# Late weight pieces rounded on ScalarE, an earlier read of the logits, the first gate mix by chunk, and a tile's Gram products between projections

## What is computed

```
L0 attention (gated delta rule, 4 heads of 32, chunks of 32 tokens):
  q, k, v = silu(conv4(x @ W.T))            # k and q then scaled to unit length
  beta = sigmoid(x @ Wb.T)
  attn = -(beta*k @ k.T) strictly lower; row by row: attn[i] += attn[i] @ attn; attn += I
  per chunk: u_new = attn @ (beta*v) - (attn @ (beta*k)) @ S
             o = q @ S + causal(q @ k.T) @ u_new;  S += k.T @ u_new
  mix = sigmoid(x @ Wmix.T);  o = mix*o + (1-mix)*v;  rms norm;  @ Wo.T
L0 feed-forward: top 2 of 8 experts by logits x @ router_w.T, softmax of the two as gate,
                 out = sum_e gate[e] * (gelu(x @ w1[e].T) @ w2[e].T)
L1 attention (linear recurrence): a = exp(-8 softplus(a_param) sigmoid(xWa)), y = scan(a, b)
L1 feed-forward: silu(xW1)*(xW2) -> gelu(.H1) -> gelu(.H2) -> W3     (128 -> 512 -> 128)
```

## Time and profile before

| | us |
|---|---|
| median of 3 runs | 802.26 |
| lowest | 798.42 |
| profiled execution | 804.78 |
| its span | 803.0 |

### The profile page before, as it was taken

One profiled execution on the slowest core, in us unless ns is written; L12 is line 12 of the kernel. 1 busy time (PEld: TensorE's weight loads), 2 busy tenths in 40 slices (PEclk: granted clock), 3 DMA queues, 4 the chain that ended last, 5 costly groups with the idle time before them and its releaser, 6 DMA issues.

```text
span 803.0 us, 11422 instructions
## 1 busy us (share of the span) xinstructions
PE 759.0 (95%) x3525; PEld 581.9 (72%) x3525; DVE 576.1 (72%) x1150; ACT 498.2 (62%) x799; POOL 491.5 (61%) x504
## 2 busy tenths in 40 slices
PE   8999999989979799999989999999999999999996
PEld 5777786777667567766777778767867787777775
DVE  5786788697669677687777777777777677776553
ACT  6877645335945565567557755774577467677753
POOL 0069699279988565987586347544754474386343
PEclk9999899789999899999999999999999999999998
DMA  4135526323131400141014002301230120021000
GB/s 144 54 106 146 168 70 180 108 80 96 37 115 51 112 14 27 53 105 28 27 53 133 27 27 63 95 26 29 63 94 24 40 65 13 1 82 39 0 14 13
DMA packets 47820, 52.68 MB, mean 66 GB/s; under 512 B 2784, under 2 KB 32224, under 8 KB 47776
## 3 DMA queue, kind: packets, MB, share of 16 engines
q1 hardware_dynamic: 47776, 52.13, 22.4%
HBM read 38.62 MB, written 13.50 MB: 65 GB/s over the span
## 4 chain that ended last, share of the span: by engine, by line
PE 67%; DVE 11%; POOL 8%; issue 6%; ACT 5%; DMA 2%; SPq 0%; DVEq 0%; ACTq 0%; POOLq 0%
PE bank L466 67%; POOL fbl L1370 3%; POOL acc L1378 2%; DVE spread L1631 1%; POOL tmp L1311 1%; POOL tpm L1314 1%; DVE sexp L1639 1%; DVE m L1688 1%; DVE x L1622 1%; DVE fbl L1838 1%; POOL texp L1338 1%; DVE yg L1649 1%; DMA conv<-in_conv 1%; DVE x3h L1855 1%; POOL fbl L1413 1%
## 5 line engine op out<-in xcount | busy, mean ns | idle before, releaser
L1370 POOL TENSOR_TENSOR fbl<-hf,fbh 128x512 fp32r<-128x512 f32 x64 | 90.2, 1409 | 40.8 <-ACT fbh L1161 40.4
L1149 ACT ACTIVATE hf<-bank 128x512 f32<-128x512 f32 x64 | 38.2, 598 | 123.0 <-PE bank L466 101.1
L1311 POOL TENSOR_TENSOR tmp<-apm,tpm 128x31 f32<-128x31 f32 (+15 forms) x124 | 73.5, 593 | 42.5 <-DVE apm L1503 34.4
L1838 DVE TENSOR_TENSOR fbl<-hf,fbh 128x512 fp32r<-128x512 f32 x64 | 69.2, 1082 | 39.4 <-ACT fbh L1155 37.1
L1314 POOL TENSOR_TENSOR tpm<-tpm,tmp 128x31 f32<-128x31 f32 (+15 forms) x124 | 77.1, 622 | 9.7
L1378 POOL TENSOR_TENSOR acc<-acc,yg 128x512 f32<-128x512 f32 x48 | 69.8, 1454 | 21.1 <-DVE yg L1649 21.1
L1413 POOL TENSOR_TENSOR fbl<-hf,fbh 128x512 fp32r<-128x512 f32 x28 | 37.0, 1324 | 72.6 <-DVE fbh L1905 72.6
L466 PE MATMUL bank<-fal,wfh 128*128 128x512 f32 x160 | 67.8, 423 | 0.0
L466 PE MATMUL bank<-fbl,wmh 128*128 128x512 f32 x128 | 60.0, 469 | 8.0 <-POOL fbl L1370 5.0
L466 PE MATMUL bank<-fah,wfh 128*128 128x512 f32 x160 | 62.5, 390 | 0.0
L466 PE MATMUL bank<-fah,wfl 128*128 128x512 f32 x160 | 62.2, 389 | 0.0
(11 more groups left out here) (246 smaller groups left out, 2155.6 us busy)
## 6 DMA issues: line engine op xcount, KB each, us to landing
gb<-gt SPq DMA_DIRECT2D x64, 256.0 KB, 3.2
pk<-pack SPq DMA_DIRECT2D x7, 1280.0 KB, 7.1
pack<-pk SPq DMA_DIRECT2D x5, 1280.0 KB, 6.9
ws<-in_wf SPq DMA_DIRECT2D x11, 256.0 KB, 2.8
pack<-pk SPq DMA_DIRECT2D x4, 640.0 KB, 4.0
xs<-in_xh SPq DMA_DIRECT2D x8, 262.0 KB, 2.8
xt<-in_xh SPq DMA_DIRECT2D x8, 262.0 KB, 2.9
ws<-in_wm SPq DMA_DIRECT2D x8, 256.0 KB, 3.3
```

Source lines behind the costliest of these rows:

```text
L1149: A.activation(hf[:, 0, :], bank[4][:, :], ACT.Gelu).then_inc(S["gelu_done"], 1)
L1311: G.tensor_tensor(m, a, r, ALU.mult).then_inc(S["t_mul"], 1)
L1370: G.tensor_tensor(fbl[:, sl, :], hf[:, 1, :], f32(fbh[:, sh, :]), ALU.subtract)\
L1838: tt(fbl[:, sl, :], hf[:, 0, :], f32(fbh[:, sh, :]), ALU.subtract).then_inc(S["lo0"], 1)
```

## The change

```diff
 def piece_high(pieces):                      # ScalarE, new
+    for p in pieces:
+        act.wait_ge(*loaded(p))
+        A.activation(high_of(p), buf_of(p)[:, :], ACT.Copy).then_inc(S["ws_act"], 1)
 
 split_pieces (VectorE):
-    V.tensor_copy(high_of(p), buf_of(p)[:, :]).then_inc(S["ws_hi"], 1)
-    dve.wait_ge(S["ws_hi"], p + 1)
+    if p < BY_SCALAR:                        # BY_SCALAR = 9
+        V.tensor_copy(high_of(p), buf_of(p)[:, :]).then_inc(S["ws_hi"], 1)
+        dve.wait_ge(S["ws_hi"], p + 1)
+    else:
+        dve.wait_ge(S["ws_act"], p - BY_SCALAR + 1)
 
 tiles 0 to 4 (TensorE):
     else:
         project(t + 1, 0)
+        project(t + 1, 1)
     gram(t, 0)
+    if t + 1 == LEAD:
+        project(t + 1, 2)
     gram(t, 1)
 ramp1 (TensorE):
-    project(s, 1)
     delta_in(a, 0)
...
     delta_turn(a, 0)
-    project(s, 2)
 
 ramp1 (ScalarE):
     heads_in(s, 1)
+    heads_in(s, 2)
...
     A.preload_act_table_set(SILU)
-    heads_in(s, 2)
+    piece_high(PIECES[s - 1][:2])
     delta_g(a, 2)
+    piece_high(PIECES[s - 1][2:])
     heads_in(s + 1, 0)
     heads_in(s + 1, 1)
+    piece_high(PIECES[s])
     delta_g(a, 3)
 ramp2 (ScalarE):
     attention_square(a)
+    piece_high(PIECES[s][:2])
     rstd_ln("1", a, 2, a4)
 ramp3 (ScalarE):
     key_spread(s, 0)
+    key_spread(s, 1)
     lru_root(m)
 dense (ScalarE), behind the activations of expert e:
+    if first and m == 0 and e in (0, 1, 3, 5):
+        p = (0, 1, 3, 5).index(e)
+        piece_high((PIECES[NT - 2][2:] + PIECES[NT - 1])[p:p + 1])
 
 VectorE:
+def mix_chunk(a, n):
+    part = lambda ap: ap.rearrange("p (b n c) -> p b n c", b=B, n=CN)[:, :, n, :]
+    if n == 0:
+        dve.wait_ge(*after("mix_act", a + 1))
+    dve.wait_ge(*after("o_copied", CN * a + n + 1))
+    stt(part(a3[:, :]), part(a4[:, :]), 1.0, part(a3[:, :]), ALU.add, ALU.mult).then_inc(S["mix_o"], 1)
+    dve.wait_ge(S["mix_o"], CN * a + n + 1)
+    i = stt(part(a1[:, :]), part(a3[:, :]), 0.5, pk[:, n:CT:CN, SV, :], ALU.mult, ALU.add)
+    if n == CN - 1:
+        i.then_inc(S["o_ready"], 1)
 ramp1 (VectorE):
     split_x(s + 1)
+    mix_chunk(a, 0)
...
     delta_out(a, 1)
+    mix_chunk(a, 1)
...
     delta_out(a, 2)
+    mix_chunk(a, 2)
...
     delta_out(a, 3)
-    mix(a)
-    mix_end(a)
+    mix_chunk(a, 3)
 ramp3 (VectorE):
     attention_low(a)
+    logits(a)                                # the copy that top_two began with
     unit_rows(s)
     lru_m(m)
-    dve.wait_ge(S["kq_done"], 2 * s + 2)
-    tt(kspread[slot(s)][1], rep(pks[s][:, 8:16, SK:SK + 1, :], 2, NH), heads(8), ALU.mult)\
-        .then_inc(S["kexp_dve"], 1)
-    top_two(a)
+    top_two(a, False)
```

More of the change, by code:

```diff
@@ L175, in loaded @@
             return S[f"ws_in{PIECE_BUF[p]}"], 16 * (PIECE_BUF[:p].count(PIECE_BUF[p]) + 1)
+        BY_SCALAR = NM + 1
         CENTRED = tuple(range((WM - O_DN) // PIECE)) + (NM,)
@@ L187, in low_of @@
             return part_of(p, wml, wfl)
-        names = """w_in cst_in conv_in0 conv_in1 conv_in2 x_in pk_half pk_stored pk_loaded tb_in fw_in ws_in0 ws_in1 ws_hi ws_lo warm_in xs_in tt_stored
+        names = """w_in cst_in conv_in0 conv_in1 conv_in2 x_in pk_half pk_stored pk_loaded tb_in fw_in ws_in0 ws_in1 ws_hi ws_act ws_lo warm_in xs_in tt_stored
             ws_sum ws_mean ws_cen s3_row s3_read cen_ready w3_scaled wo_sum wo_mean wo_cen
             wtap_f wtap_hi wtap_done xt_hi xt_ready
-            beta_proj qkv_proj qkv_act sq_done ss_done rs_ln rs_act kq_done kt_done kexp_done kexp_dve gram_done
+            beta_proj qkv_proj qkv_act sq_done ss_done rs_ln rs_act kq_done kt_done kexp_done gram_done
             bt_ready beta_tmp beta_tok_done gram_read
@@ L523, in gram @@
                 pe.wait_ge(S["kq_done"], 2 * t + 2)
-                if t == NT - 1 and g:
-                    pe.wait_ge(S["kexp_dve"], 1)
-                else:
-                    pe.wait_ge(S["kexp_done"], 2 * t + g + 1)
+                pe.wait_ge(S["kexp_done"], 2 * t + g + 1)
                 need(pe, "gram_read", 2 * (t - 1) + g + 1)
@@ L997, in delta_g, with piece_high @@
                     .then_inc(S["turn_ready"], 1)
+            def piece_high(pieces):
+                for p in pieces:
+                    act.wait_ge(*loaded(p))
+                    A.activation(high_of(p), buf_of(p)[:, :], ACT.Copy).then_inc(S["ws_act"], 1)
             act.wait_ge(S["w_in"], 32)
@@ L1656, in mix_end @@
             def mix_end(a):
-                dve.wait_ge(S["mix_o"], a + 1)
+                dve.wait_ge(S["mix_o"], a + CN)
                 stt(by_chunk(a1[:, :]), by_chunk(a3[:, :]), 0.5, pk[:, :, SV, :], ALU.mult, ALU.add)\
@@ L1716, in attention_norm, with logits @@
                 attention_low(a)
-            def top_two(a):
+            def logits(a):
                 dve.wait_ge(S["r_done"], a + 1)
@@ L1722, in top_two @@
                     .then_inc(S["lg_ready"], 1)
+            def top_two(a, read=True):
+                if read:
+                    logits(a)
                 dve.wait_ge(*after("lg_ready", a + 1))
```

## The result

The changed kernel took 804.58 us (median of 20 runs, 800.85 to 808.67); the kernel before took 800.35 us in the 20 runs beside it. The ratio is 1.0044, with a 95% interval of 1.0024 to 1.0065: 3.5 us slower (0.0044 x 800.35; 1.9 to 5.2). Ratios here leave out the few executions that took over 1.5% longer than the fastest of their kernel, as the one of 1057.01 us, and are not quotients of the medians, which lie 4.2 us apart. The forecast was 803.9 us in a range of 797 to 810, made of a median of 802.26 and a sum of +1.6 us. The time lies in the range, and the sign of the sum is right. But the starting median was 1.9 us too high and the sum 1.9 us too small (2.6 by the medians), so most of the closeness is that two errors made up for each other.

What follows compares the result with a forecast made beforehand. TensorE, busy 759.0 of 803.0 us, was taken as the bound, leaving its idle and half-rate time to win. Ramp1 +0.4, dense(0) -0.8 and ramp3 +2.0 gave +1.6 us: 803.9 for the median, range 797 to 810.

Steps and rivals of the forecast that it cites:

- the two signs of being wrong: Forecast is wrong if squares(6) ends before 125, or ScalarE idles for a weight piece with TensorE waiting behind it.
- Three other signs: Wait at delta_x(0,2) gone; at delta_x(1,1) down from 3.03 to 2.2 us; ramp3's long wait of 4 us still there.
- Rival 1: Ramp1: the clock stays high, giving -2.3 us, 800.0 (798.7 if ramp3's chain is also covered); chance 0.35.
- the difference of 5.1 us between the two clocks in ramp1: Ramp1: -3.5 us at full rate, +1.6 with the clock lost for the whole stretch; +0.4 was taken.
- The Gram order: +3.2 forecast: Ramp1, tile 4's Grams between tile 5's projections: -0.7 us at full rate, 4.4 later if the clock falls, held likelier.
- had slack: Ramp1, VectorE: solve_out(0) and delta_x were both 2.4 us early, so the unit rows stay at 99.55.
- The casts: -3.6 forecast: Casts leaving VectorE: -2.8 us in ramp1 (wait at delta_x(0,2) and half rate behind it gone), -0.8 in dense(0).
- ramp3: +2.0 forecast: ScalarE's key spread delays heads_in(7,2), gram(7,0) and the tanh by 1.7 us, up to 3.6 if the clock falls.
- The mix by chunk: nothing forecast: End of ramp1: the mix can end 1.3 us sooner, but norms_exp is no earlier than ramp1: nothing of its own.
- Waits for weight pieces on ScalarE: ScalarE's ten casts wait for pieces: six laid bare 16.8 us, 819, chance 0.02; one or two 808 to 810, 0.08.
- The base: Start of the sum: one profiled execution of 804.78 us, moved down 2.5 to the median of three runs, 802.26.

Runs made afterwards that it cites:

- the filled kernel: Changed kernel plus 7 products that nobody reads ahead of delta_state(0,0) and 6 ahead of gram(5,0): 804.53 us, ratio 1.0048.
- the early Gram alone: Casts and mix by chunk as in the change, ramp3 as before, three projections moved ahead but gram(4,1) ahead of project(5,2): 800.14 us, ratio 0.9974.

## Why the prediction was right, and where it was not

**Forecast against its steps.** The order of events was as written: gram(4,1), heads_in(5,0), the wait of 1.77 us at delta_state(0,0), gram(5,0) at 102.3, half rate from 98.3 to 108.5 (forecast about 100 to 108), and none between 82 and 92. Neither of the two signs of being wrong came: squares(6) ends behind 128 us, and ScalarE waited for no weight piece. Three other signs failed: the wait at delta_x(0,2) stayed, the one at delta_x(1,1) went altogether, and the long wait in ramp3 shrank. Rival 1, the clock staying high, did not happen in the profiled execution of the change nor in those of ramp3 undone, of the casts undone and of the Gram order alone. The unread products show that it would have paid nothing by itself: with the clock kept in the profile the median stayed at 804.5, where rival 1 had 798.7 to 800.0. This is the step whose reason failed, the difference of 5.1 us between the two clocks in ramp1 (delta_state(0,1) at 112.8 or 107.6 us). It started at 110.85 with the clock lost and at 109.10 with it kept, because at full clock TensorE waits instead: in the filled kernel 0.69 us for the split of tile 6's x and 1.84 for VectorE's spread. Of 5.1 us, 1.7 were left at delta_state(0,1), 1.0 at delta_state(0,2) and 0.6 at up(0,0).

**The Gram order: +3.2 forecast; +4.1 measured alone, +2.2 and +4.6 beside the casts without and with ramp3.** The sum compared with one profiled execution, in which the clock had fallen at 85.1 and gram(4,1) took 3.37 us. Measured so, moving it behind two projections cost VectorE nothing (unit rows at 99.55 and 99.50), and the prediction wrote that solve_out and delta_x "had slack". The executions differ in this: in the profile with the Gram order undone the clock is 1.00 there, solve_out starts at 87.64, the unit rows at 96.76 and delta_state(0,2) at 113.85 (119.39 in the change). From its timeline of VectorE:

```profile
87.64 2.18 DVE L1532 STREAM_TRANSPOSE ttp<-tpm 128x1024 f32<-128x1024 f32 x1 [0.22 <-POOL tpm L1327]
...
96.76 0.85 DVE L1484 TENSOR_TENSOR pk<-k,hf 128x512 f32<-128x512 f32 x1
```

The slack was the half rate of that execution, not the program's.

**The casts: -3.6 forecast, -2.7 to -3.5 measured, but in another place.** The sum had -2.8 in ramp1 and -0.8 in dense(0). The wait at delta_state(0,2) is there still with the casts and mix (0.89 us in their profile, 1.09 in the change's), and missing only in the casts alone, whose profile shows none. The sum had counted all 1.06 us as gone although it had delta_x(0,2) only 0.9 us sooner. The half rate at 119.3 that the sum took with it can't be credited to the casts: ramp3 alone, without them, has the wait (1.04 us) and no half rate there. Its profile is the fair one to compare ramp1 with: delta_state(0,3) starts at 123.93 there, at 123.10 with the casts and mix and at 122.02 with the casts alone, so the casts gave 0.8 to 1.9 us in ramp1, not 2.8. In dense(0) the term was 2.4 to 3.0 and not 0.8 us, since VectorE's two subtractions also lost their collision with GpSimd. Their 1.78 and 1.66 us stood in the trace of before beside 0.68 for the same operations elsewhere, and I had not looked at why. That the total came out near is luck: of its two terms one was too big and the other too small.

**ramp3: +2.0 forecast; +3.2 measured alone, +2.4 and +4.9 beside the casts without and with the Gram order.** The first steps are right: wait ahead of gram(7,0) forecast some 2.5 us, measured 2.19; chain from up(1,0) to delta_state(2,0) forecast +1.7 to +3.6, measured +1.8 in the change's profile and +3.0 in that of ramp3 alone. I took a value near the lower end, with the reason that the store of the first half is what delta_x waits for. That reason failed: with gram(7,1) at half rate VectorE is held by the gate turn, and fbl doesn't wait for the store any more. What the sum did not have is the half rate later on (241.7 to 245.1 in the change, 236.5 to 239.9 with the Gram order undone), behind a wait of 1.47 us for VectorE. In these two profiles the next stage, from delta_state(2,0) to the first product of the second feed-forward part, took 42.7 us, and in the others 39.6 to 40.6. That this late fall comes from ramp3 is not shown: the three other profiles with the changed ramp3 (alone, casts undone, filled) do not have it.

**The mix by chunk: nothing forecast, nothing that shows** (0.9956 against 0.9957). **Waits for weight pieces on ScalarE: nothing,** and the copies took 0.61 to 0.65 us, all in time that ScalarE had.

**The base.** 1.9 us of the forecast's closeness is the median of three runs (802.26) against that of twenty (800.35). A sum from one execution of before carries the half-rate stretches of that execution, at 85, 119, 143, 167 and 228 us. The profiles of kernels with the same program in those places lack some of them, as below.

## What to carry to other kernels

Where two chains end close together, repair both or neither. The unread products alone, and the early Gram alone, brought 0 and under 1 us; together they brought 2.2 us by the medians and 3.7 by the ratios. Where the executions of one kernel spread by 10 us, compare the mean granted clock of all of them, before and after, and not only two profiles. Before a slack is read from one execution, see whether the clock had fallen in it: a slack inside a half-rate stretch can be gone in the next run. And when an operation takes 1.7 us in some places and 0.7 in others (the 64 fbl subtractions of VectorE in the change's page have a mean of 1.10), look at what the neighbour engine does at its start, because moving it by 0.5 us may be worth more than removing it.

## What the runs showed of the hardware

A VectorE subtraction with two operands in SBUF that starts 0.3 us behind a GpSimd operation of the same kind ends 0.55 us behind that one, at 1.66 to 1.78 us instead of 0.68. If it starts 0.15 us ahead, it keeps its 0.68 us, and GpSimd's addition takes 1.68 instead of 1.41. The 1.78 and 1.66 us are in all four profiles without the casts, and the same two subtractions take 0.7 us in all ten with them.

The granted clock did not follow from the order of the products alone. Five profiles have the Gram order of before, with the same wait of 1.14 to 1.19 us ahead of gram(4,0). In four of them the clock fell to 0.50 at 85.1 to 85.9 us, in the fifth (the Gram order undone) it stayed at 1.00. The wait of 3.0 us in dense(0) had half rate behind it in the kernel before (167.0 to 173.8) and with the casts undone (from 163.9), and none in ramp3 alone nor in the Gram order alone. Two places were regular. In all five profiles with the emptied gap ahead of delta_state(0,0) (waits of 1.75 to 2.07 us) the clock fell to 0.50 between 98.3 and 100.3 us, and in neither of the two with unread products in it. And in all eight profiles with the wait of 4.0 us ahead of delta_state(2,0) the clock fell within it or behind it, from 218.2 to 228.5 us.
